# Layernorm in two halves of sixteen tiles, unrolled, in a four-layer single-core kernel

## The reference

```python
def _layernorm(x, axis=-1, eps=1e-05):
    m = jnp.mean(x, axis=axis, keepdims=True)
    v = jnp.var(x, axis=axis, keepdims=True)
    return (x - m) / jnp.sqrt(v + eps)
...
    xn = _layernorm(x, axis=-1)
    x = x + _L0_attn_ref(xn, ...) + _L0_ffn_ref(xn, ...)
    xn = _layernorm(x, axis=-1)
    x = x + _L1_attn_ref(xn, ...) + _L1_ffn_ref(xn, ...)
...
```

## Time and profile before

| | us |
|---|---|
| median of three runs | 2684.47 (2677.25 to 2685.04) |
| the profiled execution | 2675.91 |
| its span, from the first to the last instruction | 2674.0 |
| busy in the span: PE / DVE / ACT / POOL | 2335.6 / 1675.1 / 1321.7 / 908.2 |

### The profile page before, as it was taken

The page is one execution under the profiler, slowest core; times in us unless marked ns, Lnnn a source line. Parts: engine busy times, 40 slices in busy tenths (PEclk is TensorE's granted clock), DMA queues, the critical chain, the costliest instruction groups (busy, mean ns, idle before and its releaser), DMA issues. The chain is left out here.

```text
span 2674.0 us, 49158 instructions
## 1 busy us (share of the span) xinstructions
PE 2335.6 (87%) x16668; PEld 1384.3 (52%) x16668; DVE 1675.1 (63%) x4898; ACT 1321.7 (49%) x2678; POOL 908.2 (34%) x1060
## 2 busy tenths in 40 slices
PE   4579998998999999999999659699999997689885
PEld 2346666996766666766766446322222223333332
DVE  7646664221666666655666666488888882678895
ACT  2136664443666666665666524146666665323322
POOL 1036664442556733332333314111111110034462
PEclk9679999998999999999999869779999999899998
DMA  6211113103011100000000006201111100000001
GB/s 156 103 50 31 32 32 82 33 29 127 17 32 16 32 4 2 17 2 18 2 2 2 3 11 194 86 19 32 33 35 33 45 19 3 33 0 0 0 0 32
DMA packets 77831, 93.67 MB, mean 35 GB/s; under 512 B 10066, under 2 KB 56163, under 8 KB 75923
## 3 DMA queue, kind: packets, MB, share of 16 engines
q1 hardware_dynamic: 64098, 77.23, 9.6%
q0 software_dynamic: 13488, 13.28, 2.5%
HBM read 54.55 MB, written 35.53 MB: 34 GB/s over the span
## 5 line engine op out<-in xcount | busy, mean ns | idle before, releaser
L957 ACT ACTIVATE WA<-a_E 128x1024 f32<-128x1024 f32 (+3 forms) x384 | 301.3, 815 | 162.0 <-PE a_E L896 123.5
L613 ACT COPY a1b_PT<-a1b_T 128x512 f32<-128x512 f32 (+3 forms) x288 | 153.7, 534 | 203.3 <-PE a1b_T L524 203.3
L434 POOL TENSOR_SCALAR XR<-XR,a1b_rinv 128x384 f32<-128x384 f32 (+1 forms) x192 | 161.9, 855 | 265.2 <-DVE a1b_rinv L686 264.9
L514 PE MATMUL a1b_S<-a1b_Kf,a1b_Qf 64*128 64x512 f32 (+3 forms) x1164 | 242.0, 521 | 0.0
L539 PE MATMUL a1b_O<-a1b_PT,WA 128*64 128x128 f32 x3456 | 225.8, 277 | 14.8 <-ACT WA L617 14.8
L681 DVE COPY a1b_PT<-a1b_T 128x128 f32<-128x128 f32 (+3 forms) x288 | 140.6, 488 | 154.0 <-PE a1b_T L524 153.8
L872 PE MATMUL a_S<-a_KS,a_QS 54*128 54x512 bf16 (+3 forms) x768 | 205.2, 354 | 33.1 <-DVE a_mx L993 19.3
L539 PEld LDWEIGHTS a1b_O<-a1b_PT,WA 128*64 128x64 f32 x3456 | 186.0, 137 | 81.8 <-ACT a1b_PT L613 39.7
L434 POOL TENSOR_SCALAR WA<-WA,a1b_rinv 128x128 f32<-128x128 f32 (+1 forms) x194 | 121.3, 638 | 214.7 <-DVE a1b_rinv L686 214.7
L872 PEld LDWEIGHTS a_S<-a_KS,a_QS 54*128 54x128 bf16 x768 | 60.4, 94 | 237.4 <-DVE a_mx L993 132.0
L604 ACT ACTIVATE XR<-XR,a1b_nmax 128x384 f32<-128x384 f32 (+1 forms) x192 | 168.1, 881 | 3.2
(11 more groups left out here) (430 smaller groups left out, 5098.6 us busy)
## 6 DMA issues: line engine op xcount, KB each, us to landing
WA<-in_w SPq DMA_DIRECT2D x8, 1024.0 KB, 10.1
a_QS<-qstack SPq DMA_DIRECT2D x32, 216.0 KB
a_KS<-kstack SPq DMA_DIRECT2D x32, 216.0 KB
a1b_tb<-tab SPq DMA_DIRECT2D x12, 512.0 KB, 4.6
qstack<-f_parts SPq DMA_DIRECT2D x24, 256.0 KB, 4.0
kstack<-f_parts SPq DMA_DIRECT2D x24, 256.0 KB, 4.1
f_slots<-f1r_zrows SPq DMA_DIRECT2D x9, 516.0 KB, 6.5
f1t_xs<-f_slots SPq DMA_DIRECT2D x9, 516.0 KB, 6.0
```

The costliest lines, as they stand in the source:

```text
L434: pool.tensor_scalar(soft(i0, u), soft(i0, u), rinv[:, n:n + 1], 1.0, ALU.mult, ALU.mult).then_inc(n_sb, 1)
L514: pe.matmul(pS[k % NB][:, 0:hi - lo], Qf[half, b0 % 2, i0 * P:(i0 + 1) * P], Kf[half, b0 % 2, lo:hi], start=True, stop=True).then_inc(s_ps, 1)
L613: act.copy(PT[:, i % 2 * HG + u, lo:hi], pT[0][:, 0:hi - lo]).then_inc(t_sb_a, 1)
L957: act.activation(PT[:, q % NP, :, off:CH], pE[q % 2][:, :, off:CH], ACT.Exp).then_inc(e_sb, 1)
```

## The change

`layernorm` alone is changed, and with it all four calls. The 32 tiles are cut into two halves of 16, and both of DVE's loops and ACT's loop are written out. DVE's new order is: statistics of half 0, its seven small instructions, 4 statistics of half 1, `rstd` of half 0, 4 more statistics, the 16 scalings of half 0, the last 8 statistics, the seven small instructions of half 1, its `rstd`, and its 16 scalings. ACT takes the root of half 0, four copies, the root of half 1, and four copies. PE has four PSUM buffers in place of two. The work of SP and POOL is as it was.

```diff
-    pst = [ph.ps(f"t{i}") for i in range(2)]
+    H = NT // 2
+    NB = 4
+    pst = [ph.ps(f"t{i}") for i in range(NB)]
...
-            with dve.Fori(0, NT // CT) as c:
-                for k in range(CT):
-                    ins = dve.bn_stats(stats[:, c * CT + k, :], X[:, c * CT + k, :])
-                ins.then_inc(stats_done, 1)
...
-            with dve.Fori(0, B) as b:
-                for h in range(2):
-                    for k in range(CT):
-                        n = b * TT + (h * CT + k)
-                        ins = dve.tensor_scalar(XR[:, n, :], X[:, n, :], mean[:, bass.ds(n, 1)], rstd[:, bass.ds(n, 1)],
-                                                ALU.subtract, ALU.mult)
-                    ins.then_inc(xn_done, 1)
...
+            statistics(range(H)).then_inc(stats_done, 1)
+            moments(0)
+            statistics(range(H, H + 4))
+            inverse(0)
+            statistics(range(H + 4, H + 8))
+            scaled(0)
+            statistics(range(H + 8, NT)).then_inc(stats_done, 1)
+            moments(1)
+            inverse(1)
+            scaled(1)
...
+            deviation(0)
+            for c in range(NT // CT):
+                b, h = divmod(c, TT // CT)
+                if c == H // CT:
+                    deviation(1)
+                act.wait_ge(tr_done, c + 1)
+                act.copy(XNT[:, b, 1 + h * CH:1 + (h + 1) * CH], pst[c % NB][:, :]).then_inc(out_done, 1)
...
-                if c >= 2:
-                    pe.wait_ge(out_done, c - 1)
+                if c >= NB:
+                    pe.wait_ge(out_done, c - NB + 1)
```

More of the change, by code:

```diff
@@ L135, in layernorm, with scale @@
     stats = ph.sb("stats", [P, NT, 6])
[L136 to L142, removed]
+    mean, half, sq, m2, var, sd, rstd = (ph.sb(n, [P, NT]) for n in ("mean", "half", "sq", "m2", "var", "sd", "rstd"))
     XR = G["XR"]
-    pst = [ph.ps(f"t{i}") for i in range(2)]
+    H = NT // 2
+    NB = 4
+    pst = [ph.ps(f"t{i}") for i in range(NB)]
     stats_done, mv_done, sd_done, rstd_done = (ph.sem(n) for n in ("stats", "mv", "sd", "rstd"))
-    xn_done, tr_done, out_done = (ph.sem(n) for n in ("xn", "tr", "out"))
+    xn_dve, tr_done, out_done = (ph.sem(n) for n in ("xndve", "tr", "out"))
+    def scale(engine, n):
+        return engine.tensor_scalar(XR[:, n, :], X[:, n, :], mean[:, n:n + 1], rstd[:, n:n + 1], ALU.subtract, ALU.mult)
     with nc.Block() as block:
@@ L172, in _, with statistics @@
-            dve.wait_ge(rstd_done, 1)
-            with dve.Fori(0, B) as b:
-                for h in range(2):
-                    for k in range(CT):
-                        n = b * TT + (h * CT + k)
-                        ins = dve.tensor_scalar(XR[:, n, :], X[:, n, :], mean[:, bass.ds(n, 1)], rstd[:, bass.ds(n, 1)],
-                                                ALU.subtract, ALU.mult)
-                    ins.then_inc(xn_done, 1)
+            def statistics(tiles):
+                for n in tiles:
+                    ins = dve.bn_stats(stats[:, n, :], X[:, n, :])
+                return ins
@@ new lines, in moments @@
+            def moments(h):
+                cut = slice(h * H, (h + 1) * H)
+                dve.wait_ge(stats_done, 3 * h + 1)
+                dve.tensor_tensor(mean[:, cut], stats[:, cut, 1], stats[:, cut, 4], ALU.add)
+                dve.tensor_tensor(half[:, cut], stats[:, cut, 1], stats[:, cut, 4], ALU.subtract)
+                dve.tensor_tensor(m2[:, cut], stats[:, cut, 2], stats[:, cut, 5], ALU.add).then_inc(stats_done, 1)
+                dve.wait_ge(stats_done, 3 * h + 2)
+                dve.tensor_scalar(mean[:, cut], mean[:, cut], 0.5, None, ALU.mult)
+                dve.tensor_tensor(sq[:, cut], half[:, cut], half[:, cut], ALU.mult)
+                dve.tensor_scalar(m2[:, cut], m2[:, cut], 4.0 / P, None, ALU.mult).then_inc(stats_done, 1)
+                dve.wait_ge(stats_done, 3 * h + 3)
+                dve.tensor_tensor(var[:, cut], sq[:, cut], m2[:, cut], ALU.add).then_inc(mv_done, 1)
@@ new lines, in inverse, with scaled @@
+            def inverse(h):
+                cut = slice(h * H, (h + 1) * H)
+                dve.wait_ge(sd_done, h + 1)
+                dve.reciprocal(rstd[:, cut], sd[:, cut]).then_inc(rstd_done, 1)
+            def scaled(h):
+                dve.wait_ge(rstd_done, h + 1)
+                for c in range(h * H // CT, (h + 1) * H // CT):
+                    for n in range(c * CT, (c + 1) * CT):
+                        ins = scale(dve, n)
+                    ins.then_inc(xn_dve, 1)
+            statistics(range(H)).then_inc(stats_done, 1)
@@ L181, in _, with deviation @@
+            moments(0)
[7 more added lines that the diff above has]
+            scaled(1)
         @block.scalar
         def _(act):
[L183 to L188, removed]
+            def deviation(h):
+                cut = slice(h * H, (h + 1) * H)
+                act.wait_ge(mv_done, h + 1)
+                act.activation(sd[:, cut], var[:, cut], ACT.Sqrt, bias=G["eps"][:, 0:1], scale=0.25).then_inc(sd_done, 1)
@@ L192, in _ @@
             for c in range(NT // CT):
-                pe.wait_ge(xn_done, c + 1)
-                if c >= 2:
-                    pe.wait_ge(out_done, c - 1)
+                pe.wait_ge(xn_dve, c + 1)
+                if c >= NB:
+                    pe.wait_ge(out_done, c - NB + 1)
                 for k in range(CT):
-                    ins = pe.transpose(pst[c % 2][:, k * P:(k + 1) * P], XR[:, c * CT + k, :], G["ident"][:, :])
+                    ins = pe.transpose(pst[c % NB][:, k * P:(k + 1) * P], XR[:, c * CT + k, :], G["ident"][:, :])
                 ins.then_inc(tr_done, 1)
```

## The result

| | us |
|---|---|
| before, median of six runs | 2679.91 (2675.05 to 2685.04) |
| changed, median of six runs | 2662.20 (2660.54 to 2665.73) |
| ratio of the runs | 0.994 (95% interval 0.9929 to 0.995) |
| profiled execution, span: before / changed | 2674.0 / 2660.8 |

The account below looks back on a forecast made before the run. DVE's chain from statistics through scalings to the last transposes and copy was taken to bound each layernorm. Gains of 3 x 2.9 us (n1 to n3) and 4.4 (n0) took 13 off a middle of 2681: 2668, range 2656 to 2680.

Parts of the forecast that it names:

- Statistics without the loop: DVE's statistics in each layernorm, written out, start 0.189 us apart in place of 0.229; half 0 takes 3.1 us.
- rival B: Unrolled layernorm statistics stay 0.229 us apart, so only 8 us off in all, or 5; chance 0.10.
- Small instructions: DVE's short instructions between statistics and root, now run twice per layernorm, take 1.13 us for each half.
- Scaling: DVE's unrolled scalings in each layernorm start 0.258 us apart, so half 0's 16 take 4.1 us.
- Rival A: Unrolled layernorm scalings start 0.19 us apart, up to 2.6 us more per layernorm, 23 us off in all; chance 0.14.
- Before the second scaling: In half 1, from `n_var` to the first scaling, uncovered: 0.70 us in place of 1.12.
- Tail: From half 1's first scaling to the end of the last copy: 6.1 us with slow matmuls, 5.65 with fast ones.
- Rival E: Half 0's copies lag by over 0.8 us and delay half 1's root; some 9 us gain at 1 us lag; chance 0.05.
- n0: First layernorm gains 4.4 us; its last copy ends near 34.2, just after SP's transfers at 33.9.
- rival D: Fetching some 320 written-out DVE instructions delays each; at 0.1 us each the kernel is 19 us slower; chance 0.04.
- rival C: Run times fall on two levels some 8 us apart; mostly on the upper, 13 us gain becomes 5; chance 0.12.
- the phases stay as they are: Behind the layernorms' barriers, the other phases stay unchanged, each beginning with PE at rest before and after.

Follow-up runs that it names:

- e2_loops_halves: The kernel before with its loops kept, but cut into halves in the changed kernel's order, two PSUM buffers as before; 2676.52 us, 0.9987 of before.
- three kernels with delays: The changed kernel with 46, 6 or 12 more statistics, which nobody reads, ahead of the first in n0; spans 2668.5, 2663.6 and 2662.2 us.
- in one piece: The changed kernel without its halves: 32 statistics, one set of small instructions, 32 scalings, still unrolled; 2656.51 us, 0.990 of before.

## Why the prediction was right

The mechanism was right: DVE's chain sets the length of each layernorm, and unrolling shortens it. The forecast was a gain of 13 us over the profiled execution, and the spans differ by 13.2; but that match is partly luck: the layernorms gave 15.4, and other phases took back 2.2. The forecast time, 2668, is 5.8 us above the measured 2662.20, though inside its range. It started from a middle of 2681 and took 13 off, while the medians lie 17.7 apart. Term by term:

- *Statistics without the loop.* 16 in 3.19 us, (3.19 - 0.276) / 15 = 0.194 apart, where 0.189 was taken from moe_join. Right; rival B, with 0.229, falls.
- *Small instructions.* From 81.86 to 82.85, 0.99 us in each half where 1.13 was kept: the figure for 32 columns was kept, and it was 0.14 too high, twice. This is the largest part of what the sum, 19.6 us, has over the measured 19.13.
- *Half 0's root and reciprocal covered.* No idle time on DVE before the first reciprocal. Scaling of half 0 began 5.76 us in (5.9 forecast).
- *Scaling.* 0.256 apart (0.258). Rival A, with 0.19, falls. Right, but the reason was only an analogy to front's row. The estimate of 0.127 us from the Trainium skill ("VectorE: DVE Perf Modes", section "The TRN2 errata — SBUF-src ops pay a fixed extra latency per instruction"), which the prediction had set aside, is near the form without per-row scalars, 0.136; the 0.06 us for each of them is not in that formula.
- *Before the second scaling.* From 91.15 to 91.82, 0.67 us (0.70). The loop entry was what filled the 0.37 us between reciprocal and scaling of before: where `e2_loops_halves` keeps the loop it is 0.37 again.
- *Tail.* 5.98 us (6.1) at the slow pace, in every layernorm, as forecast for two separate bursts. It is no rule for this form: in five of the six n0 and n3 of the three kernels with delays, the part behind the last scaling was 1.40 to 1.67 us in place of 1.79.
- *Order on ACT.* The fourth copy ended at 90.40 and `n_var` at 91.15: 0.75 us of slack (0.8). Rival E falls.
- *Start.* DVE's first statistics came 0.03 us after ACT's table load in place of 0.34; 0.27 was taken. In n2 they came 0.68 earlier than before, 0.4 more than that.
- *n0.* The last copy ended at 33.74, SP's last issue at 26.71 + 6.92 = 33.63 us: just not the bound, as the sum said. Where the copies end earlier, in one piece, SP is the bound.
- *Instruction supply (rival D).* No idle "issue" time within the straight rows, in n0 under the stream of weights either.
- *Two levels of the whole time (rival C).* They don't show. The six runs of the changed kernel lie within 5.2 us (2660.54 to 2665.73), and 17 runs of the kernel before, beside the first experiments, are spread from 2672.39 to 2685.76, with seven of them between 2678 and 2682.

What the working missed is the step "the phases stay as they are". They hold their instructions but not their time: the matmul clock moves moe_tiles and the second attention by 2 to 3.4 us from execution to execution, as much as one layernorm gained, and wkv moves by 3.4 for a reason that stays open. It also took the halves as given, and never priced one unrolled piece, which needs 0.85 us less of DVE.

## What to carry to other kernels

Overlap inside an engine-bound phase is worth only what it takes off the engine that bounds it; splitting a chain in two to let others start early adds work to that very engine, and may break up the others' bursts. Written-out code in place of short hardware loops was worth 4.4 us a phase here (22.22 to 17.82), of which the halves gave 1.3 away; moving a share to an idle engine was worth 1 to 1.5 more, although DVE then took longer for each instruction. On short instructions, count operands: each per-row scalar cost 0.06 us, where the whole instruction without any took 0.22.

## What the runs showed of the hardware

- A per-row scalar adds 0.06 us to a DVE `tensor_scalar` of 128x128 float32 (0.218, 0.282, 0.341 us with none, one and two).
- `bn_stats` starts 0.23 us apart in a loop with register instructions and 0.19 in straight code, and a loop's turn adds 0.22 us more (kernel before, n1).
- Through 12.20 us of matmuls with 8 columns, one behind the other, PE busy for 12.20 of them, the granted clock stays at 0.50. It had been at the full level until about 0.4 us after their start, with 1.81 us of idle time just before them; which of the two let it fall is not shown.
- The same kernel had moe_tiles at 197.5 and 195.6 us, at a granted clock of 0.55 and 0.77 in its first 15 us.
- DVE and POOL scaling beside each other: 0.391 us for DVE in place of 0.341; POOL took 0.838 for one.
